# Row factors of scaled queries stored by even and odd heads; the second chunk's statistics ahead of the first mask

## The reference

```python
ig = (x @ Wi + bi); fg = (x @ Wf + bf)          # x = [q, k, v] side by side
log_f_cum = cumsum(log_sigmoid(fg))             # along the sequence
log_D = tril(log_f_cum - log_f_cum^T) + ig^T
D = exp(log_D - max(log_D)); C = (q @ k^T) / sqrt(64) * D
h = C / (max(|sum(C)|, exp(-max(log_D))) + 1e-6) @ v
x = x + tanh(g_xattn) * norm_of_each_head(h) * ln_scale
```

## Time and profile before

| | us |
|---|---|
| median of 3 runs | 3248.26 (3246.73 to 3250.17) |
| profiled execution, its own time | 3251.57 |
| its span | 3250.0 |
| TensorE busy | 2989.3 (92%) |
| VectorE, ScalarE, GpSimd busy | 1647.2, 1013.8, 588.7 |

### The profile page before, as it was taken

One profiled execution on the slowest core, in us unless ns is written; L12 is line 12 of the kernel. 1 busy time (PEld: TensorE's weight loads), 2 busy tenths in 40 slices (PEclk: granted clock), 3 DMA queues, 4 the chain that ended last, 5 costly groups with the idle time before them and its releaser, 6 DMA issues.

```text
span 3250.0 us, 50376 instructions
## 1 busy us (share of the span) xinstructions
PE 2989.3 (92%) x17262; PEld 2465.7 (76%) x17263; DVE 1647.2 (51%) x3107; ACT 1013.8 (31%) x1916; POOL 588.7 (18%) x572
## 2 busy tenths in 40 slices
PE   3788888988888888699999999999999999999999
PEld 3677776777777766488888888888888888888887
DVE  3777766677777765433333333333333334444444
ACT  4434333333334332223233333333333231111111
POOL 1233332333323333000000000000000001111111
PEclk8799999999999999799999999999999999999999
DMA  6455444444444542423333342442242334444444
GB/s 177 137 143 145 137 138 131 125 131 124 131 125 135 147 127 74 161 86 136 136 136 136 139 167 106 169 173 99 103 172 101 132 136 136 155 140 157 148 143 149
DMA packets 227240, 441.93 MB, mean 136 GB/s; under 512 B 86784, under 2 KB 112256, under 8 KB 226560
## 3 DMA queue, kind: packets, MB, share of 16 engines
q1 hardware_dynamic: 202704, 367.18, 35.1%
q0 software_dynamic: 24400, 72.96, 6.8%
HBM read 350.72 MB, written 107.18 MB: 141 GB/s over the span
## 4 chain that ended last, share of the span: by engine, by line
PE 56%; DVE 1%; ACT 1%; issue 0%; DMA 0%; ACTq 0%; DVEq 0%; POOLq 0%
PE p_g_b L1506 18%; PE p_up_b L1506 18%; PE p_y_b L1494 16%; PE p_x_b L1474 3%; PE p_h_b L1481 1%; DVE w_lo_b L1344 1%; ACT w_hi_b L1287 1%; DMA xg_b<-mid_xn,idx_b 0%; ACTq L1145 0%; DMA idx_b<-mid_lists 0%; ACTq L1130 0%; DVE r_b L1400 0%; DVE sg_b L1372 0%; DVE r_b L1391 0%; ACT th_b L1329 0%
## 5 line engine op out<-in xcount | busy, mean ns | idle before, releaser
L1506 PE MATMUL p_g_b<-w_hi_b,xt_hi_b 128*128 128x512 f32 x840 | 339.2, 404 | 20.2 <-DVE w_lo_b L1344 18.3
L1360 DVE TENSOR_TENSOR ht_lo_b<-p_h_b,ht_hi_b 128x512 fp32r<-128x512 f32 x105 | 72.5, 691 | 539.2 <-ACT ht_hi_b L1299 539.2
L1494 PE MATMUL p_y_b<-w_hi_b,ht_hi_b 128*128 128x512 f32 x840 | 336.0, 400 | 1.9 <-DVE ht_lo_b L1360 1.9
L1506 PE MATMUL p_g_b<-w_hi_b,xt_lo_b 128*128 128x512 f32 x840 | 328.8, 391 | 0.0
L1506 PE MATMUL p_up_b<-w_lo_b,xt_hi_b 128*128 128x512 f32 x840 | 328.7, 391 | 0.0
L1506 PE MATMUL p_up_b<-w_hi_b,xt_lo_b 128*128 128x512 f32 x840 | 328.4, 391 | 0.0
L1506 PE MATMUL p_up_b<-w_hi_b,xt_hi_b 128*128 128x512 f32 x840 | 328.1, 391 | 0.0
L1494 PE MATMUL p_y_b<-w_hi_b,ht_lo_b 128*128 128x512 f32 x840 | 327.4, 390 | 0.0
L1494 PE MATMUL p_y_b<-w_lo_b,ht_hi_b 128*128 128x512 f32 x840 | 327.2, 390 | 0.0
L1506 PE MATMUL p_g_b<-w_lo_b,xt_hi_b 128*128 128x512 f32 x840 | 326.9, 389 | 0.0
L1372 DVE SCALAR_TENSOR_TENSOR sg_b<-th_b,p_g_b 128x512 f32<-128x512 f32 x105 | 72.3, 688 | 491.5 <-ACT th_b L1329 491.5
(11 more groups left out here) (222 smaller groups left out, 5732.8 us busy)
## 6 DMA issues: line engine op xcount, KB each, us to landing
mid_y<-y_b SPq DMA_DIRECT2D x73, 512.0 KB, 3.2
x<-in_x SPq DMA_DIRECT2D x64, 512.0 KB, 3.9
gbd<-mid_g_row SPq DMA_DIRECT2D x64, 512.0 KB, 5.7
stage_b<-in_eg SPq DMA_DIRECT2D x16, 2048.0 KB
stage_b<-in_eu SPq DMA_DIRECT2D x16, 2048.0 KB, 15.3
stage_b<-in_ed SPq DMA_DIRECT2D x16, 2048.0 KB, 19.5
mid_y<-in_x SPq DMA_DIRECT2D x34, 512.0 KB, 5.5
ctx_t<-in_ctx_t SPq DMA_DIRECT2D x32, 512.0 KB, 6.8
```

Source lines behind the costliest of these rows:

```text
L1360: nc.vector.tensor_tensor(ht_lo[:, :, :], p_h[:, :, :], ht_hi[:, :, :].bitcast(f32), ALU.subtract).then_inc(ht_rdy, 1)
L1494: last = nc.tensor.matmul(p_y[n][:, :], a[:, k, :], b[:, GUP + k, w], start=(k == 0 and m == 0), stop=(k == FE // P - 1 and m == 2))
L1506: mm = nc.tensor.matmul(out[:, :], a[:, k, :], w[:, k, o:o + FE], start=(k == 0 and m == 0), stop=(k == KD - 1 and m == 2))
```

## The change

Three edits.

1. The view of `mid_s_row` in memory is split as (o k) instead of (k o): the factors of the even heads lie in its first 8 rows, those of the odd heads in the last 8. SyncE writes them with two DMAs of 8 rows (from every other partition of `rows`), where one DMA of 16 rows did it. The counts of the semaphore `s_out` go from 16 to 32 a chunk.
2. The two loads of `qs_t` then read one run of 8 x 512 B = 4 KB for each partition. Bytes and number of issues are as before.
3. In `AHEAD`, ("L", 1, 1), ("Q", 1, 1), ("Q", 2, 1), ("Q", 3, 1) move up ahead of ("A", 7, 0), and ("L", 1, 1) ahead of ("A", 5, 0).

```diff
-        s_rows = t["s_row"].rearrange("(k o) s -> o k s", o=2)
+        s_rows = t["s_row"].rearrange("(o k) s -> o k s", o=2)
...
         AHEAD = (("T", 1, 0), ("L", 1, 0), ("Q", 1, 0), ("Q", 2, 0), ("Q", 3, 0), ("X", 1, 1), ("A", 1, 0),
-                 ("T", 1, 1), ("W", 0, 0), ("A", 2, 0), ("A", 3, 0), ("A", 4, 0), ("A", 5, 0), ("A", 7, 0), ("L", 1, 1),
-                 ("Q", 1, 1), ("Q", 2, 1), ("Q", 3, 1), ("X", 1, 2), ("A", 8, 0), ("A", 9, 0))
+                 ("T", 1, 1), ("W", 0, 0), ("A", 2, 0), ("A", 3, 0), ("A", 4, 0), ("L", 1, 1), ("A", 5, 0),
+                 ("Q", 1, 1), ("Q", 2, 1), ("Q", 3, 1), ("A", 7, 0), ("X", 1, 2), ("A", 8, 0), ("A", 9, 0))
...
-                        sp.dma_start(t["s_row"], rows[:, 3, :]).then_inc(s_out, 16)
+                        for o in range(2):
+                            sp.dma_start(s_rows[o], rows[o:NH:2, 3, :]).then_inc(s_out, 16)
...
-                    sp.wait_ge(s_out, 16 * n + 16)
+                    sp.wait_ge(s_out, 32 * n + 32)
                     for o in range(2):
-                        sp.dma_start(qs_t[DH * o:DH * o + DH, :, :], s_rows[o].partition_broadcast(DH)).then_inc(sf_in, 16)
+                        sp.dma_start(qs_t[DH * o:DH * o + DH, :, :].rearrange("p k s -> p (k s)"),
+                                     s_rows[o].rearrange("k s -> (k s)").partition_broadcast(DH)).then_inc(sf_in, 16)
...
-                        ge(dve, s_out, 16 * scaled_before(b, j))
+                        ge(dve, s_out, 32 * scaled_before(b, j))
```

## The result

| | before | changed |
|---|---|---|
| median of 13 runs, us | 3247.93 (3244.26 to 3254.97) | 3255.30 (3248.91 to 3263.94) |
| ratio, 95% interval | | 1.0024 [1.0015, 1.0032] |
| profiled execution | 3251.57 | 3250.97 |

The changed kernel is **slower** by 7 to 8 us. The forecast was 3215.3 and the range 3192 to 3246: too fast by 40 us, and outside the range. The profiled execution of the changed kernel happens to be one of its fastest, so the two profiles by themselves show no difference in time. What they show is where the expected gain is not.

What follows compares the result with a forecast made beforehand. The prediction took TensorE's mixer stall behind the `qs_t` load as the bound. It summed -7.7 (start), -20 (4 KB runs less the extra issue) and -5 (clock) to -33 us: 3215.3 us, range 3192 to 3246.

Steps and rivals of the forecast that it cites:

- What bounds the kernel: In the mixer, TensorE stalls 3.7 us each on ScalarE's `q_t`, which follows the DMA load of `qs_t`; 77.4 us in 21 waits.
- a stall is worth its length: In the mixer, the chain behind the `qs_t` load moves TensorE one for one while the stall lasts.
- Part 1: At the start, GpSimd's second-chunk power ahead of the first masks brings later work forward: -7.7 us, bounds -9 and -3.
- Part 2: In 24 chunks, the factors' write in two issues delays `qs_t` by 0.54 us a chunk, bounds 0.3 and 0.9.
- Part 3: Loading `qs_t` in 4 KB runs shortens its transfer by 1.4 us a chunk; net of the extra issue, -20 us.
- 128 packets of 4 KB take 1.3 us: New `qs_t` transfer behind `ctx_v`, from stretches where 97 and 103 such packets start in a us.
- the 1024 packets of 512 B: Old `qs_t` transfer, taken to need 2.5 to 3.4 us, from stretches starting 408 and 304 packets a us.
- `gbd` at 111 GB/s: Slow row for 4 KB runs from one place, lower bound for the `qs_t` transfer: a loss of 2.3 us.
- Part 4: In the mixer, shorter stalls reduce TensorE's time at half clock by 0.22 us a chunk: -5 us, bounds 0 and -20.
- The issue's length: The `qs_t` issue on SyncE stays some 4 to 5 us long, since it waits for `ctx_v` to drain.
- the run's length doesn't matter: Rival: the `qs_t` transfer saves nothing and the extra issue stays, +8 us in all, 3256.5; chance 0.09.
- faster: Whole kernel faster by more than 0.2%, 6.5 us: the forecast, the "more" rival and half the write-cost rival; chance 0.77.

Runs made afterwards that it cites:

- e20: Changed kernel with both factor writes behind `mid_g_row`, the `ctx_v` load behind `qs_t` and the `xn` store behind that: 3119.99 us, 0.9626 of the kernel before.
- e3: Kernel before with the factors written by two DMAs of 8 rows into the old layout, loads and start unchanged: 3274.38 us, ratio 1.0099.
- e10: Kernel before with a second write of all 16 factor rows to memory that nobody reads: 3253.28 us, ratio 1.0044.
- e1: Kernel before with only the new `AHEAD` order at the start: 3234.49 us beside 3241.64, ratio 0.9976.
- e2: Changed kernel with the old `AHEAD`, so only the new layout, two writes and 4 KB runs: 3260.05 us, 1.0049 of the kernel before.
- e5: Changed kernel with the factors written by one DMA of 16 rows whose destination is stepped: 3231.99 us, 0.9971 of the kernel before.
- e22: Changed kernel with `qs_t` loaded from 64 different rows of `x`, factors not applied: 3231.40 us, 0.9971 of the kernel before.
- e18: Changed kernel with `qs_t` loaded by one DMA to all 128 partitions, all getting the even heads' factors: 3223.90 us, 0.9945 of the kernel before.
- e14: Kernel before with the new start and the `ctx_v` load behind `qs_t`; 512 B runs, one plain write: 3149.84 us, ratio 0.9722.
- e7: Changed kernel with only the `ctx_v` load moved behind those of `qs_t`: 3165.09 us, 0.9772 of the kernel before.
- e13: Changed kernel with one stepped 16-row write, placed behind `mid_g_row`, and the `ctx_v` load behind `qs_t`: 3129.22 us, 0.9646 of the kernel before.
- e16: Changed kernel with one stepped 16-row write and the `ctx_v` load behind `qs_t`: 3134.75 us, 0.9681 of the kernel before.
- e4: Changed kernel with the two 8-row writes moved behind `mid_g_row`, ahead of the wait for its landing: 3214.68 us, 0.9898 of the kernel before.
- e19: Changed kernel with `qs_t` loaded by four DMAs of 32 partitions, the halves in turn: 3235.45 us, 0.9978 of the kernel before.

## Why the prediction failed, step by step

- **What bounds the kernel:** right. The stall behind `qs_t` is the mixer's bound; every run that moved the load moved the time the same way, and e20, which took the stall away, stands at 0.9626. Worth less than right: "a stall is worth its length". An issue that stands in the chain was worth 1.3 times its length (e3: 1.1 to 1.5; e10: 0.8 to 1.8).
- **Part 1:** right, -7.7 forecast and -7.8 measured (e1, -4 to -11), with `q`, the copy and the masks within 0.3 us of the times given.
- **Part 2:** the mechanism right, the term mis-sized: 0.54 forecast, 1.02 measured. I had taken the price of a 16-row issue for an issue of 8 rows, and the bounds, 0.3 and 0.9, did not reach the truth: both came from the same row, and an operation that the trace does not show (a DMA from every other partition, with 8 rows) may cost more than the one it replaces, not only less. A better bound from above was in the rows: `ctx_v`'s issue, another shape on the same queue, stands for 0.63, and two such in place of one of 0.34 are 0.92 more, with the gap between them about the 1.02.
- **Part 3: the step that failed.** The transfer was to save 1.4 us a chunk and saved 0.4 to 0.5 (e2 with e3, e5 with e1; 5.5 to 5.0 us in the table). The term "128 packets of 4 KB take 1.3 us" was wrong: they took 2.6 to 2.9 in every kernel, behind `ctx_v`, behind `xn` or into an empty queue. I had the 97 and 103 packets a us from 432:433 and 551:552 without asking whose they were. Counted in order, 432:433 is mostly the store of `xn` and 551:552 mostly the second half of `gbd`. The other term was off as well: the 1024 packets of 512 B took 4.4 us from first to last, not 2.5 to 3.4. The row that came near the truth is the one that I dismissed, `gbd` at 111 GB/s: its first 128 packets of 4 KB take 3.0 us, its second 128 take 1.4. My reason, a queue that had just started, can't be the whole, since `qs_t` is as slow in a running queue. Why one load of 4 KB packets is slow and the next fast stays open; the source's rows (e22) and the halves of partitions (e18) don't change how fast the packets start.
- **Part 4:** -5 forecast, and nothing of it is there: the mean clock of the changed kernel is 0.95 as before. It had the stall shorten, and the stall grew. In e3, with the longest stalls, the clock was 0.93.
- **The issue's length** (4 to 5 us) stayed as forecast, 4.69.

With the measured terms the sum is -7.8 + 31 x (1.02 - 0.47) = +9, where 31 is 24 chunks at the price of 1.3. Measured were +7.4 and +12. Of the rivals the one that came nearest in time, "the run's length doesn't matter" (+8, 3256.5), had other terms: the runs were worth a half us and the write cost twice as much. It had 0.09; that its time was near is luck in part, since its two errors offset each other. The two terms that decided between it and the forecast (a rate and an issue) rested on rows of other operations, and 0.77 for "faster" was far too sure for that.

## What to carry to other kernels

Before taking a DMA's rate from a stretch, count through the queue whose packets they are: packets of one size can be another transfer's, even a store's. What a load waits before its first packet is a term of its own, and here it was the larger one. On a queue in a chain without gaps, ask first in which order things are issued: putting the large load of small packets behind the small urgent one was worth 82 to 94 us here (e14, e7, e13 and e16 against the same kernels without it), the longer runs 16 at best. An extra issue cost next to nothing where the queue waits for a landing anyway (e4, e20), and some 1.3 times its length in front of that (e3).

## What the runs showed of the hardware

- A write of 8 rows of 512 B held SyncE 0.66 us, one of 16 rows 0.34, one of 16 rows through a stepped destination 0.73 (e3, e10, e5).
- The 128 packets of 4 KB of `qs_t` took 2.6 to 2.9 us to start, 44 to 49 a us, behind 2048 packets of 256 B (changed kernel), behind a store in packets of 4 KB (e13) and into an empty queue (e20, about half of its chunks). In the same queue the second half of `gbd` ran at 91 a us (128 in 1.4 us, before). The source's rows make no difference (e22). Why it is so, and why four loads of 32 partitions were faster than two of 64 (e19), no run settled.
- Behind a load of 2048 packets of 256 B the next issue stood for 3.6 to 5.6 us in the chunks shown (changed kernel, e20). Without that load ahead the two issues of `qs_t` took 1.15 us together (e13).
- In a mixer with a stall of 3 to 4 us in every chunk, 1 us of issue more a chunk cost 1.3 us (e3, 1.1 to 1.5), and the mean granted clock of the stretch went with it: 0.93 with the longest stalls (e3), 0.95 before, 0.99 without them (e20).
